# Where in the attention's steps each small piece of work stands: new offsets and a new order inside a step

## The reference, cut to what matters

```python
q = (x @ Wq).reshape(b, T, 32, 8).transpose(0, 2, 1, 3)   # 32 heads of 8
k = (x @ Wk).reshape(b, T, 8, 8).transpose(0, 2, 1, 3)    # 8 key heads, 4 query heads to each
v = (x @ Wv).reshape(b, T, 8, 8).transpose(0, 2, 1, 3)
q, k = _apply_rope(q, cos, sin), _apply_rope(k, cos, sin)
scores = einsum('bkgtd,bksd->bkgts', qg, k) / sqrt(8)      # causal, T = 256
attn = softmax(scores, axis=-1)
ctx = einsum('bkgts,bksd->bkgtd', attn, v)
return ctx @ Wo + b_out
```

## Time and profile before

| | |
|---|---|
| time, median of 3 runs | 654.26 us (653.88 to 654.45) |
| the profiled execution's own time | 658.78 us |
| its span | 657.0 us |
| granted TensorE clock, mean | 0.995 |
| busy in the span: PE, DVE, ACT, POOL | 627.3, 531.1, 423.2, 331.5 us |
| instructions | 14843 |

### The profile page before, as it was taken

How to read it: one execution, slowest core, us unless ns; L and a number is a source line. 1 busy time by engine, 2 the same in 40 slices (tenths; PEclk the granted TensorE clock), 3 DMA queues, 4 the chain that set the end, 5 groups by cost and what they waited for, 6 DMA issues and landing times.

```text
span 657.0 us, 14843 instructions
## 1 busy us (share of the span) xinstructions
PE 627.3 (95%) x5678; PEld 523.6 (80%) x5678; DVE 531.1 (81%) x1055; ACT 423.2 (64%) x798; POOL 331.5 (50%) x528
## 2 busy tenths in 40 slices
PE   8987899999999879999979999999999999999995
PEld 6854566666666558888879999999999999888884
DVE  5889999999998724679768888888988888558886
ACT  2547888899888964442347876787877787422322
POOL 3427577888766751101345454444454430078854
PEclk9999999999999999999999999999999999999998
DMA  4864335565520000000376786877776764032311
GB/s 149 155 119 92 68 91 101 100 140 139 108 60 20 12 17 16 9 1 14 127 261 211 245 281 212 275 236 258 241 265 235 260 219 153 25 90 83 94 56 64
DMA packets 79669, 87.11 MB, mean 133 GB/s; under 512 B 54224, under 2 KB 69072, under 8 KB 79600
## 3 DMA queue, kind: packets, MB, share of 16 engines
q0 software_dynamic: 11872, 54.53, 25.2%
q1 hardware_dynamic: 67312, 31.12, 19.6%
q10 hardware_dynamic: 416, 0.52, 0.3%
HBM read 63.87 MB, written 9.31 MB: 111 GB/s over the span
## 4 chain that ended last, share of the span: by engine, by line
PE 81%; DVE 9%; ACT 3%; issue 3%; POOL 2%; another core or an unknown queue 1%; DMA 1%; POOLq 0%; SPq 0%; DVEq 0%; ACTq 0%
PE PS L562 77%; DVE NM L1086 3%; PE PS L573 2%; DVE NM L1082 2%; PE PS L773 1%; ACT PF L935 1%; ACT WH L882 1%; POOL PF L1504 1%; DMA X<-in_x 1%; PE PS L721 1%; POOL RS L1447 0%; DVE RR L1047 0%; DVE RA L1040 0%; PE PS L819 0%
## 5 line engine op out<-in xcount | busy, mean ns | idle before, releaser
L1291 DVE TENSOR_TENSOR HF<-SS,PS 128x256 f32<-128x256 f32 (+2 forms) x141 | 68.7, 487 | 71.0 <-ACT SS L981 38.7
L1370 DVE TENSOR_TENSOR WL<-RAW,WH 128x768 fp32r<-128x768 f32 x125 | 118.5, 959 | 4.2 <-ACT WH L882 3.7
L981 ACT ACTIVATE SS<-PS 128x256 f32<-128x256 f32 (+2 forms) x141 | 62.0, 440 | 85.3 <-PE PS L562 69.6
L562 PE MATMUL PS<-WH,HH 128*128 128x256 f32 x355 | 103.4, 291 | 3.6 <-DVE HL L1384 3.4
L1504 POOL TENSOR_SCALAR_AFFINE_SELECT PF<-PF 128x512 f32<-128x512 f32 x128 | 84.5, 685 | 41.3 <-ACT PF L935 41.3
L882 ACT ACTIVATE HH<-HF 128x256 fp32r<-128x256 f32 (+1 forms) x120 | 58.0, 483 | 72.0 <-DVE HF L1291 65.7
L882 ACT ACTIVATE WH<-RAW 128x768 fp32r<-128x768 f32 x125 | 103.3, 841 | 0.0
L562 PE MATMUL PS<-WL,HH 128*128 128x256 f32 x355 | 100.4, 283 | 0.0
L562 PE MATMUL PS<-WH,HL 128*128 128x256 f32 x355 | 100.3, 282 | 0.0
L935 ACT ACTIVATE PF<-PS 128x1536 f32<-128x1536 f32 x64 | 92.8, 1449 | 9.8 <-PE PS L562 9.0
L562 PE MATMUL PS<-XGL,WH 128*128 128x256 f32 x320 | 91.1, 285 | 0.0
(11 more groups left out here) (212 smaller groups left out, 1526.1 us busy)
## 6 DMA issues: line engine op xcount, KB each, us to landing
ys<-YO SPq DMA_DIRECT2D x16, 256.0 KB
RAW<-in_wsh SPq DMA_DIRECT2D x4, 768.0 KB, 4.7
XT<-in_xt SPq DMA_DIRECT2D x8, 256.0 KB, 3.1
X<-in_x SPq DMA_DIRECT2D x8, 256.0 KB, 4.5
xn<-YY SPq DMA_DIRECT2D x16, 128.0 KB, 1.7
out<-X SPq DMA_DIRECT2D x15, 128.0 KB
ys<-YO SPq DMA_DIRECT2D x7, 128.0 KB
RAW<-in_wsh SPq DMA_DIRECT2D x2, 384.0 KB, 5.1
```

The source lines that it names most:

```text
L562: return eng.matmul(o, l, r, start=start, stop=stop, skip_group_check=True)
L981: eng.activation(ss, both(i, bank(b))[0], ACT.Silu).then_inc(free[b] if dense(i) else silu, 1)
L1291: eng.tensor_tensor(hf, ss, both(c, bank(b))[1], ALU.mult).then_inc(free[b], 1)
L1370: eng.tensor_tensor(WL[q % 2][:, c], RAW[raw_of(q)][:, c], WH[q % 2][:, c].bitcast(F32), ALU.subtract).then_inc(w_lo, 1)
```

## The change

It alters five tables of numbers and the order of the tokens, and no instruction.

```diff
-FRONT = {"f_split": -88, "f_stats": -96, "f_dev": -93, "f_qkv": -78, "f_taken": -78, "f_rope": -74, "f_first": -69, "f_second": -67, "f_third":
-         -63, "q": -59, "k": -57, "k_first": -68, "k_third": -64, "f_fourth": -62, "k_twice": -61}
-FRONT0 = {"f_stats": -108, "f_dev": -111, "f_qkv": -87, "f_taken": -87, "f_rope": -83, "f_first": -81, "f_second": -80,
-          "f_third": -77, "q": -77, "k": -74, "k_first": -81, "k_third": -80, "f_fourth": -77, "k_twice": -73}
-FRONT1 = {"f_stats": -98, "f_dev": -95, "f_qkv": -77, "f_taken": -78, "f_rope": -78, "f_first": -78, "f_second": -71, "f_third":
-          -68, "q": -60, "k": -59, "k_first": -77, "k_third": -71, "f_fourth": -67, "k_twice": -66}
-BACK = {"b_turn": 46, "b_turned": 45, "b_out": 53, "b_taken": 54, "b_dev": 55, "b_add": 57, "b_stats2": 61, "b_dev2": 63,
-        "b_norm2": 66, "b_turn2": 70, "b_high": 69, "b_low": 68, "b_route": 75, "b_kept": 73}
-STATS = ((4, -50), (5, -48), (6, -46), (7, -44), (8, -42), (9, -40))
-ORDER = "x a 2 b d l s1 s0 m0 s2 w m1 v t V m2 m3 s3 T W"
+FRONT = {"f_split": -86, "f_stats": -95, "f_dev": -96, "f_taken": -78, "f_qkv": -80, "f_rope": -76, "f_third": -61,
+         "f_first": -69, "f_second": -67, "q": -62, "k": -68, "k_first": -66, "f_fourth": -62, "k_third": -64,
+         "k_twice": -61}
+FRONT0 = {"f_stats": -116, "f_qkv": -89, "f_first": -78, "f_rope": -83, "f_dev": -118, "f_third": -74, "f_taken": -87,
+          "f_second": -77, "q": -77, "k": -71, "k_first": -79, "k_third": -80, "f_fourth": -73, "k_twice": -73}
+FRONT1 = {"f_stats": -98, "f_dev": -97, "f_qkv": -77, "f_taken": -79, "f_rope": -78, "f_first": -78, "f_second": -72,
+          "k_first": -76, "f_third": -64, "k": -62, "q": -48, "k_third": -68, "k_twice": -58, "f_fourth": -68}
+BACK = {"b_out": 53, "b_turn": 44, "b_turned": 47, "b_taken": 52, "b_dev": 53, "b_add": 56, "b_stats2": 61, "b_dev2":
+        60, "b_norm2": 66, "b_turn2": 70, "b_low": 68, "b_high": 69, "b_kept": 72, "b_route": 75}
+STATS = ((4, -50), (5, -46), (6, -43), (7, -42), (8, -42), (9, -40))
+ORDER = "a 2 b x d l s1 s0 s2 w m0 t m1 m2 m3 v T V W s3"
```

## The result

The changed kernel takes 661.95 us (median of 5 runs, 660.59 to 664.21), the kernel before in the same rounds 654.26 us (653.85 to 654.45). The ratio is 1.0118, 95% interval [1.0103, 1.0133]: +7.7 us. I had forecast 654.6 us and a range up to 657.2.

The account below looks back on a forecast made before the run. The prediction took PE and VectorE, both full from 98 to 187 us, as the bound. Its terms, -0.2 + 1.0 + 0.3 - 0.6 + 0.7 - 0.9 = +0.3 us on 654.26, gave 654.6 us, range 651.6 to 657.2.

Parts of the forecast that it names:

- PE's list: PE's pieces: claimed to come out the same from first to last, with the same ring banks.
- the three order edits: `exp` behind `pass2`, `weigh` ahead of `m0`, `turn` ahead of `back`: claimed to cost and bring nothing.
- Part 1: First batches: the first two tiles' DMAs are issued some 0.6 us sooner; -0.2 us.
- Part 2: SP's early queue: q of tile 3 behind the constants lands later and delays pair 8's maxima; +1.0 us.
- Part 3: SP's steady queue: k ahead of q, both ahead of the pair; +0.3 us, from -0.3 to +3.0.
- three times 1.0: Upper bound of Part 3: PE's three waits for the pair, nothing absorbed; +3.0 us.
- Part 4: VectorE's new step order: sooner divide -0.6, adjacent statistics and `f_dev` +0.7, third step away from GpSimd's zeroing -0.9 us.
- the -0.6 for the divide: Term of Part 4: `divide` some 0.4 us sooner shortens PE's bank wait and VectorE's XL wait; bounds 0 and -0.9.
- Slower, by SP's queue alone: Rival: q of tile 3 and the steady pairs go out late; +2.4 us, 656.7 us; chance 0.25.
- Nothing: Rival: the list differs but each queue's waits end where they did; 654.3 us; chance 0.14.
- faster: Rival: VectorE's third and fourth steps both come down to their least; -2.9 us, 651.4 us; chance 0.27.

Follow-up runs that it names:

- h1: The changed kernel with the steady part's loads of x transposed and x issued behind the pair of maxima; 1.0033 of the kernel before.
- h2: h1 with the early stage's q and k (tiles 2 and 3) placed as in the kernel before; 1.0033 became 0.9996 of the kernel before.
- e3: The kernel before with q of tiles 2 and 3 behind the first maxima's pair, tile 3's also behind a load and five constants; ratio 1.0029.
- e4: The kernel before with SyncE's new steady order alone: k, the loads, memory write, q, pair; ratio 1.0102.
- e2: The kernel before with SyncE's whole list as in the changed kernel, other engines' lists old; ratio 1.0131.
- g1: The kernel before with k ahead of q in the steady part: memory write, k, the loads, q, pair; ratio 1.0068.
- g3: e4 with the loads issued behind the pair: k, memory write, q, pair, loads; 0.9987 of the kernel before.
- h4: g3 with VectorE's third step moved behind the fourth step and the divide; 0.9987 of the kernel before.
- h3: h2 with VectorE's third step ahead of the divide again in the steady part; 1.0013 of the kernel before.
- g4: The kernel before with only the steady part's two loads issued behind the pair: write, q, k, pair, loads; ratio 0.9993.
- g2: The kernel before with the steady SyncE order k, the loads, pair, q; ratio 1.0006.

## Why the prediction was wrong, by its own steps

**What bounds the kernel: half right.** Both engines are full in that stretch, as the earlier trace rows show. From that I concluded that an order could only win or lose what the two engines themselves lose. The pair's transfers were the third thing near its limit: the earlier trace rows showed 1.1 us of waiting for them in three places, which says that they had no slack there, and I read it as a small number.

**PE's list, and the three order edits: right.** No trace shows a loss of theirs. h1 and h2 carry all the new lists of ScalarE, VectorE and GpSimd, and h2 is at 0.9996.

**Part 1, early tiles: nothing visible.** The first exponential starts at 43.31 us instead of 43.16; I had -0.2. k of tile 1, the last of the four DMAs, went out at 21.72 us, and at 21.71 in the kernel before.

**Part 2, q of tile 3: mechanism right, first half right, size wrong.** Predicted: issued 42.9, landed 48.0, maxima of pair 8 at 48.6. Measured: issued 43.28, landed 4.7 us later, and the maxima at 48.61, behind a PE wait for QT<-QC. The second pair, which I had at 51.1, went out at 51.79, since the q ahead of it took 3.23 us to issue; nothing waited for it. The term was +1.0 with an upper bound of 1.9; e3 and the difference of h1 and h2 give 1.9 and 2.4 us, with wide intervals. What I left out is that a delay of one DVE piece shifts its neighbours against GpSimd's. From the maxima of pair 8 to the third maxima behind it the kernel before took 7.64 us (47.63 to 55.27), the changed one 8.21 (48.61 to 56.82), +0.57: the scaling of WO took 0.64 instead of 0.42 and RR 0.81 instead of 0.47. In h2, with q early and GpSimd's list that of the changed kernel, both are back at 0.42 and 0.47. (The rotary product's 1.12 us beside GpSimd's L1516, 50.29 to 51.37, is no part of it: in the kernel before two other rotary products were as much longer.) PE's idle time ahead of the `late` products grew from 1.49 to 2.50 us. The clock fell behind it in the changed kernel and not in e3, where PE idled 2.54 us; by the eighth exponential the changed kernel is 3.0 us late, e3 2.0 and h1 1.5, so the clock's share of this term stays open.

**Part 3, k ahead of q: the step that failed.** The term was +0.3, bounds -0.3 to +3.0; measured, 5.6 us by h1, 6.7 by e4. I wrote the sequence "k then takes 1.3 us, the write 0.4, q 1.4 to 3.0", and so put the pair out at 126.6 to 128.2 instead of 127.53. For that tile it was right: its pair went out at 131.12 us, which is 127.1 less the 4.0 us by which the execution was late there. But it is a tile without loads, and it was made to stand for all. Two things are wrong for the others. In every second tile the loads stand between k and q, 1.1 us that I left out of the sum although its first sentence names them. And the length of q behind them is not drawn from 1.4 to 3.0: in the four kernels with that order (changed, e2, e4, g1) all 16 of those q, 12 behind both loads and 4 behind XT alone, took 2.97 to 3.67 us, while the 12 steady ones of g3 took 1.50 to 2.26. At the three places behind both loads the pair went out 1.4, 1.7 and 2.0 us later than in the kernel before, the lateness of the execution taken off. Then the size: "three times 1.0" assumed that only the places that waited before would wait. Such a pair made four places wait, up to 2.4 us, and six in e4.

**Part 4, VectorE's steps: three terms, net -0.8, measured nothing.** The third step did come down: in the changed kernel 415 ns at the least, 416 in the median and 426 at the most, where the earlier trace rows had 407, 544 and 700; that was predicted to the hundredth. Statistics and aggregate in a row took 0.55 us, 125.97 to 126.52, as I had reckoned. But the three together bought no time: free of the loads and of q the whole measures 0.9996 (h2) against 0.9987 (g3, with VectorE's old list). Of the third step alone two pairs of runs say different things: with the old lists its new place is worth nothing (h4 and g3, both 0.9987), with the new ones 0.17%, 1.1 us (h2 against h3). The earlier divide did cut PE's wait for it, from 3.4 us to 1.8, but turned into a wait for the product ahead of it. Waits over the steady stretch of the changed kernel:

```profile
DVE NM L1083 <- PE PS L563: 3.2, 5, 1.9
DVE RC L1096 <- PE PS L574: 1.6, 2, 1.4
DVE XL L1363 <- ACT XH L883: 0.7, 4, 0.2
```

The wait of XL is 0.7 us where it was 0.9, and RC, which did not wait in the kernel before, waits 1.6: the -0.6 for the divide seems to have gone there. That part is read from the rows and not tested alone.
On the overlap, the Trainium skill, page "SBUF — State Buffer", section "Who interferes with whom", has the right pairs of instructions: a VectorE operation with two SBUF inputs beside GpSimd's reads. Here they stretched by 0.12 us (L1067, 534 ns on the mean against 415) and by 0.77 (RB, 1.12 against 0.35); only the second is as long as a full block would make it.

**The rivals.** "Slower, by SP's queue alone" named the mechanism, the place and the point of decision (pairs later by half a microsecond) and was priced at +2.4 us; it happened at +7.7. It had 0.25. Its price was low for the reasons given under parts 2 and 3, and the clock, which the sum did not have at all, may have taken a share (below). "Nothing" and "faster" fell.

**What I said would show it.** q3 at 43 us and the maxima at 48.6: seen. PE's wait for QT<-NMT between 0.8 and 2.6 us: it was 5.4, and this alone refutes part 3. The stretch from 98 to 187 us in 88 to 89: it took 92.22. "The stretch behind 240 us has another length" came true (417.0 us before, 411.8 after) through the execution of before, not through the change.

## What to carry to other kernels

A transfer of a few kilobytes whose wait already shows in the trace, however small the number, has no slack: count every issue that an edit puts ahead of it on its queue, and take the length of each issue from rows with the same neighbour ahead of it, in each kind of tile, not from one tile and not from the range over all rows. Put loads that nobody waits for behind it; here that alone turned +1.0% (e4) into -0.1% (g3). An instruction that grew shorter on a full engine is no gain before the one that took its place has been read.

## What the runs showed of the hardware

- A DMA_TRANSPOSE holds SyncE's queue for a time that hangs on what went ahead: k's took 1.23 to 1.28 us as the first after a pause in most rows of these kernels and 1.30 to 1.98 behind a q, once 3.25 (g4); q's 1.50 to 2.26 behind k (g3), 2.97 to 3.67 behind one or both loads of 256 KB. Only the last held in every row: without loads ahead some q took 2.7 to 3.4 us too (h1's at 101.46: 3.08, h3's at 164.75: 3.36, and in the kernel before the 2.97 of the earlier trace rows), three in g2, behind the pair and a load of 384 or 768 KB, took 3.9 to 4.9, and what they have in common is not found. The Trainium skill, page "DMA: Bandwidth & Descriptors", section "Issuing engines are not separate DMA queues", calls the time to initiate a DMA "usually small relative to the DMA itself". The trace disagrees for these: 2.57 us to issue (median of the changed kernel's q) against 4.8 from issue to landing.
- TensorE's granted clock fell to the lower of its two levels within attention in some executions. In the changed kernel that was at 55.32 us, behind the 2.50 us that PE stood idle up to 54.56:

```profile
50.00:56.00 6.00, 3.50 (x60) 1.90 (x56) 5.83 (x12) 3.83 (x5) 5.73 (x8) 0.94 0.71 90
56.00:62.00 6.00, 5.57 (x45) 3.54 (x42) 5.58 (x11) 3.68 (x8) 1.48 (x3) 0.50 0.00 0
```

  In the second window the clock is 0.50, that is 1.2 GHz; the six products of 128x384 took 2.29 us, in the kernel before 1.34. It fell again at 150.89 us, behind the wait of 2.14 us, and from the 32nd exponential to the 34th the changed kernel lost 3.3 us against the kernel before. The length of the idle time just ahead does not decide it: in g2, g4, h3 and h4 the clock fell near 55 us too, behind 1.48 or 1.49 us, where the kernel before idled 1.49 and kept it; and it did not fall in e3 behind 2.54 us, nor in e4's profile with six waits up to 2.8 us.
- So a wait can cost more than itself, in some executions. In e4's twelve it can be read off: the five with a mean granted clock of 0.996 to 0.998 took 658.82 to 661.30 us, the seven with 0.983 to 0.991 took 663.71 to 668.57. The fifteen executions of the kernel before at 0.996 and above, in the same rounds, had a median of 655.78. So the order on SyncE costs e4 some 4.8 us at the full clock (medians, 660.62 against 655.78), and the slow clock comes with 4.9 more. The five of the changed kernel are too few to part its 7.7 us so: 661.95 us at 0.996, 660.59 to 664.21 at 0.985 to 0.990.
